# Last stages of three groups moved into the last group's recurrence, with its key-value products on GpSimd

## The reference, cut to what matters

```python
def step(s, rkvw):
    r_t, k_t, v_t, w_t = rkvw
    a = k_t[..., :, None] * v_t[..., None, :]          # product of keys and values
    out = jnp.einsum('bhi,bhij->bhj', r_t, u * a + s)
    s = a + w_t[..., :, None] * s
    return (s, out)
...
x1 = x + og * g @ Wo.T
xc = _ln(x1, ln2_w, ln2_b)
sx2 = jnp.concatenate([state[:, 0:1] - xc[:, :1], xc[:, :-1] - xc[:, 1:]], axis=1)
xk2 = xc + sx2 * ffn_maa_k
xr2 = xc + sx2 * ffn_maa_r
rr = jax.nn.sigmoid(xr2 @ Wfr.T)
kk = jnp.square(jax.nn.relu(xk2 @ Wfk.T))
return x1 + rr * (kk @ Wfv.T)
```

## Time and profile before

| | us |
|---|---|
| median of the runs | 2015.81 |
| the profiled execution, whole | 2021.98 |
| its span, first to last instruction | 2020.2 |
| TensorE (PE) busy | 1784.4 (88%) |
| VectorE (DVE) busy | 1176.1 (58%) |
| ScalarE (ACT) busy | 637.1 (32%) |
| GpSimd (POOL) busy | 223.3 (11%) |
| mean granted TensorE clock | 0.92 |

### The profile page before, as it was taken

The page is one execution under the profiler, slowest core; times in us unless marked ns, Lnnn a source line. Parts: engine busy times, 40 slices in busy tenths (PEclk is TensorE's granted clock), DMA queues, the critical chain, the costliest instruction groups (busy, mean ns, idle before and its releaser), DMA issues.

```text
span 2020.2 us, 18127 instructions
## 1 busy us (share of the span) xinstructions
PE 1784.4 (88%) x6760; PEld 883.8 (44%) x6760; DVE 1176.1 (58%) x1649; ACT 637.1 (32%) x1480; POOL 223.3 (11%) x317
## 2 busy tenths in 40 slices
PE   6999998999999979999999979989779889856447
PEld 3555443445554433455554433445434334422223
DVE  1233002339988853449988654279988633299951
ACT  2566211136652112246641131256621131101011
POOL 1010000122210010122110010221200101100000
PEclk9999998799999989899999988999979987967868
DMA  7000021151102122341102321430012312400011
GB/s 234 26 26 21 22 83 63 62 160 33 40 27 77 63 99 81 96 125 40 53 14 71 105 76 60 128 97 32 14 34 84 103 47 85 146 25 21 7 57 39
DMA packets 73608, 135.15 MB, mean 67 GB/s; under 512 B 16241, under 2 KB 26993, under 8 KB 73521
## 3 DMA queue, kind: packets, MB, share of 16 engines
q1 hardware_dynamic: 59808, 101.05, 15.6%
q0 software_dynamic: 10496, 29.34, 4.7%
q10 hardware_dynamic: 3216, 3.60, 0.6%
HBM read 111.95 MB, written 22.02 MB: 66 GB/s over the span
## 4 chain that ended last, share of the span: by engine, by line
PE 68%; DVE 19%; issue 5%; DMA 3%; ACT 2%; ACTq 1%; POOL 1%; SPq 0%; DVEq 0%; POOLq 0%
PE bank L270 48%; PE bank L433 10%; DVE C L1079 5%; PE bank L497 3%; DVE sm L1020 3%; DVE C L1069 2%; PE bank L312 2%; DMA ring<-in_stream 2%; DVE YB L1091 1%; PE bank L304 1%; DVE C L1083 1%; DMA s<-in_ctx 1%; PE bank L324 1%; ACT XA L809 1%; PE bank L511 1%
## 5 line engine op out<-in xcount | busy, mean ns | idle before, releaser
L270 PE MATMUL bank<-C,ring 128*128 128x448 f32 x640 | 265.2, 577 | 17.9 <-DVE C L1131 17.9
L1079 DVE TENSOR_TENSOR_SCAN C<-XA,C 128x896 f32<-128x896 f32 x112 | 222.6, 2022 | 27.5 <-ACT XA L843 27.5
L433 PE MATMUL bank<-ring,HT 128*112 128x512 f32 x512 | 222.3, 592 | 0.0
L1020 DVE CUSTOM_DVE_ANT_0 sm<-bank,maskb 112x375 f32<-112x375 f32 x256 | 124.0, 541 | 166.5 <-PE bank L304 166.5
L270 PE MATMUL bank<-ctx_t,Wk 128*128 128x375 f32 x512 | 194.3, 504 | 13.4 <-DMA Wk<-in_wk 11.0
L270 PE MATMUL bank<-SX,ring 128*128 128x448 f32 x512 | 196.8, 543 | 7.8 <-ACT SX L809 7.8
L270 PEld LDWEIGHTS bank<-C,ring 128*128 128x128 f32 x640 | 128.5, 203 | 153.5 <-issue 149.6
L270 PE MATMUL bank<-Wv,ctx_t 128*125 128x512 f32 x384 | 182.3, 600 | 0.4 <-ACT C L809 0.4
L270 PE MATMUL bank<-ring,C 128*112 128x512 f32 x256 | 129.5, 662 | 56.1 <-issue 43.6
L312 PEld LDWEIGHTS bank<-ident,sm 112*125 112x125 f32 x768 | 123.5, 192 | 122.5 <-ACT sm L824 59.1
L830 ACT ACTIVATE probT<-bank 125x336 f32<-125x336 f32 x256 | 114.0, 445 | 145.8 <-PE bank L312 143.4
(11 more groups left out here) (132 smaller groups left out, 2056.4 us busy)
## 6 DMA issues: line engine op xcount, KB each, us to landing
ring<-in_stream SPq DMA_DIRECT2D x64, 1024.0 KB, 5.5
ctx_t<-in_ctxT SPq DMA_DIRECT2D x16, 750.0 KB, 5.0
rkw_scratch<-HT POOLq DMA_DIRECT2D x48, 224.0 KB, 2.7
rkw<-rkw_scratch POOLq DMA_DIRECT2D x32, 224.0 KB, 3.1
HT<-in_x SPq DMA_DIRECT2D x16, 224.0 KB, 5.3
X<-in_x SPq DMA_DIRECT2D x16, 224.0 KB, 6.1
v_scratch<-HT POOLq DMA_DIRECT2D x16, 224.0 KB, 2.6
VB<-v_scratch SPq DMA_DIRECT2D x4, 896.0 KB, 7.1
```

The source lines that it names most:

```text
L270: last_ = nc.tensor.matmul(out_ap, pairs[k][0], pairs[k][1], start=(k == 0), stop=(k == len(pairs) - 1))
L433: last_ = nc.tensor.matmul(bank[SC[b]][0:LQ, :], HT[:, c, b * LQ:(b + 1) * LQ], w[:, c, :], start=(m == 0 and c == 0), stop=(m == 3 and c ...
L1020: nc.vector.tensor_tensor_reduce(out=sm[0:LQ, slot, :], in0=tile(name)[0:LQ, 0:LK], in1=maskb[:, n % 2, :], scale=-SCALE, scalar=3.0e38, o ...
L1079: own.step(nc.vector.tensor_tensor_scan(out=part, data0=wrep[:, i % 2, :], data1=part, initial=0.0, op0=ALU.mult, op1=ALU.add))
```

## The change

Four things change.

1. **The last stage leaves the borders.** The borders of groups 1, 2 and 3 keep only WO and the start of `pre`. For groups 0 and 1, x1 is stored to DRAM (`x1_scratch`) in place of the output, and loaded again later; the x1 of group 2 stays in SBUF. The normalised rows of `pre` get four tiles, so that they need not wait for each other, and W1 reads C[1].
2. **The last stages stand elsewhere.** They are done in the order LAST = [2, 0, 1, 3]. Numbers k below count in that order. Layer norm, mixes and FK of k = 0 stand within `pre(3)`; the table AHEAD places the rest of k = 0, and all of k = 1 and 2, between the channels of group 3's recurrence on TensorE (FV of k = 2 behind it); VectorE, ScalarE and GpSimd have their shares at fixed channels. k = 3 follows at the end, with FR ahead of FV rather than in turn with it. These stages use buffers of their own: Wk, Wv, Wq, Wc, qT, V and ctx_t, which are free by then. The normalised rows are made by ScalarE with a third small GpSimd operation (`shift`).
3. **GpSimd makes the products of keys and values in the last recurrence**, up to two channels ahead; VectorE waits for `kv_ready` in place of L1069. The final sum of the last stage is GpSimd's for k < 3.
4. ScalarE's copies of the decays during the MLP are spread in finer portions.

```diff
+LAST = [2, 0, 1, 3]
...
 def pieces_of(g):
+    if g == NG:
+        return [(kind, k) for k in range(NG) for kind in (["wo"] if k == NG - 1 else []) + ["fk", "fr", "fv"]
+                if (kind, k) != ("fk", 0)]
+    return MLP_P + ([("wo", 0)] if g > 0 else []) + PRE_P[0:2] + ([("fk", 0)] if g == NG - 1 else []) + PRE_P[2:4]
...
+AHEAD = {0: [("fr", 0, 0), ("fr", 0, 1), ("fr", 0, 2), ("fr", 0, 3)], 1: [("fv", 0, 0), ("fv", 0, 1)],
+         2: [("fv", 0, 2), ("fv", 0, 3), ("ln", 1)], 4: [("fk", 1, 0), ("fk", 1, 1)], 5: [("fk", 1, 2), ("fk", 1, 3)],
...
+         12: [("fr", 2, 0), ("fr", 2, 1)], 13: [("fr", 2, 2), ("fr", 2, 3)],
+         RS: [("fv", 2, 0), ("fv", 2, 1), ("fv", 2, 2), ("fv", 2, 3)]}
...
+            def border(g):
...
+                w = weights(g, ("wo", 0))
+                pe.wait_ge(og_ready, g)
+                recurrence_out(g, w, 0)
+                recurrence_out(g, w, 1)
+                pre_cols(g, 0)
+                pre_cols(g, 1)
+                recurrence_out(g, w, 2)
+                pre_cols(g, 2)
+                pre_cols(g, 3)
+                recurrence_out(g, w, 3)
...
                     channels_out([("P", g, j, e) for e in range(E)], w, C[j % 2])
+                    if g == NG - 1 and j == 1:
+                        last_cols(0)
+                    elif g == NG - 1 and j == 2:
+                        last_stage(g, [("fk", 0, e) for e in range(E)])
 
             def sum_channels(p):
...
                 for i in range(RS):
+                    last_stage(p + 1, AHEAD.get(i, []))
                     pe.wait_ge(scan_step, p * RS + i + 1)
...
+            def last_product(i):
+                p = NG - 1
+                pool.wait_ge(rkw_in[(i // BLOCK) % 2], 32 * (p * (RS // BLOCK // 2) + i // BLOCK // 2 + 1))
+                if i == 1:
+                    ready(pool, ("P", p, 4, E - 1))
+                elif i >= 4:
+                    pool.wait_ge(summed, i - 3)
+                kk = rkw[:, (i // BLOCK) % 2, i % BLOCK, 1, :]
+                nc.gpsimd.tensor_tensor(S_of[i % 4][:, :, 1:LQ], VB[:, :, 0:LQ - 1],
+                                        kk[:, 0:LQ - 1].unsqueeze(1).to_broadcast([P, RS, LQ - 1]), ALU.mult
+                                        ).then_inc(kv_ready, 1)
...
+                    pool.wait_ge(v_in, 80 * NG)
+                    last_product(0)
+                    last_product(1)
+                    for i in range(RS):
+                        if i in (1, 7):
+                            last_std(1 if i == 1 else 2)
+                        blocks_after(p, i * UNITS, (i + 1) * UNITS)
+                        if i + 2 < RS:
+                            last_product(i + 2)
+                        if i in (2, 9):
+                            last_add(0 if i == 2 else 1)
+                            last_store(0 if i == 2 else 1)
...
             def scan_unit(p, unit):
+                    if last:
+                        dve.wait_ge(kv_ready, i + 1)
+                    else:
+                        own.step(nc.vector.tensor_tensor(S[:, :, 1:LQ], VB[:, :, 0:LQ - 1],
...
+                    for i in range(RS):
+                        if i in (1, 7):
+                            last_stats(1 if i == 1 else 2)
+                        if i in (2, 3):
+                            last_out(0, 2 * (i % 2), 2 * (i % 2) + 2)
+                        elif i in (9, 10):
+                            last_out(1, 2 * ((i + 1) % 2), 2 * ((i + 1) % 2) + 2)
+                        if i in (4, 10):
+                            last_mixes(1 if i == 4 else 2)
+                        units(p, i * UNITS, (i + 1) * UNITS)
```

More of the change, by code:

```diff
@@ L388, in step, with weights, piece_done, channels_out @@
                     denominators(n)
-            def weights(g, k):
-                at = PIECE0[g] + k
+            def weights(g, piece):
+                at = PIECES.index((g, piece))
                 pe.wait_ge(ring_in[at % SLOTS], (at // SLOTS + 1) * 16)
                 return ring[:, at % SLOTS, :, :]
-            def piece_done(g, k):
-                piece_over[PIECE0[g] + k] = (psum_ready, tiles.done)
-            def channels_out(names, w, src, blocks=None):
+            def piece_done(g, piece):
+                piece_over[PIECES.index((g, piece))] = (psum_ready, tiles.done)
+            def channels_out(names, w, src):
                 for e in range(E):
                     k = wide()
[L401 to L406, removed]
+                    closed(product(bank[k][:, 0:T], [(w[:, c, e * P:(e + 1) * P], src[:, c, :]) for c in range(E)]),
+                           names[e], k)
             def mlp(g):
@@ L479, in pre @@
             def pre(g):
-                w0 = 8 if g == 0 else 12
-                if g == 0:
-                    ln_cols("pre", g)
                 k = wide()
@@ L565, in _ @@
                     mlp(g)
+                    border(g)
+                    pre(g)
                 else:
                     sum_channels(g - 1)
-                if g > 0:
-                    post(g)
-                if g < NG:
-                    pre(g)
+                    w = weights(g, ("wo", NG - 1))
+                    pe.wait_ge(og_ready, g)
+                    for b in range(GB):
+                        recurrence_out(g, w, b)
+                    piece_done(g, ("wo", NG - 1))
+                    last_stage(g, [("ln", NG - 1), *((kind, NG - 1, at) for kind in ("fk", "fr", "fv")
+                                                     for at in range(4))])
         @block.sync
@@ new lines, in last_keys @@
+            def last_keys(k, lo=0, hi=E):
+                for e in range(lo, hi):
+                    name = ("FK", k, e)
+                    if k > 0:
+                        ready(act, ("FV", k - 1, GB - 1))
+                    ready(act, name)
+                    nc.scalar.activation(KK[:, e, :], tile(name)[:, 0:T], ACT.Relu).then_inc(freed(name), 1)
+                for e in range(lo, hi):
+                    evacuated(act, ("FK", k, e))
+                    nc.scalar.activation(KK[:, e, :], KK[:, e, :], ACT.Square).then_inc(kk_ready, 1)
@@ new lines, in mlp_add, with pre_apply @@
+            def mlp_add(g, b):
+                name, rows = ("ACC", g, b), rows_of(g, b)
+                ready(dve, name)
+                nc.vector.tensor_tensor(rows, tile(name)[0:LQ, :], rows, ALU.add).then_inc(freed(name), 1)
+                evacuated(dve, name)
+                stats("pre", rows, b)
+            def pre_apply(g, b):
+                dve.wait_ge(rstd_ready["pre"], g * GB + b + 1)
+                nc.vector.tensor_scalar(xn_pre[b], rows_of(g, b), mv["pre"][:, b, 0:1], rstd["pre"][:, b:b + 1],
+                                        ALU.subtract, ALU.mult).then_inc(xn_ready["pre"], 1)
```

472 lines of the change are left out of this document (282 added, 190 removed), and 2 rows, old and new, of the table AHEAD.

## The result

The changed kernel takes 1942.7 us (median of 4 runs, 1927.39 to 1952.98), the kernel before, on the same chip, 2018.86 us (4 runs, 2010.25 to 2030.77): ratio 0.9613, 95% interval 0.9529 to 0.9696. The forecast was 1958 us. The profiled execution is the longest of its four, 1952.98 us with a span of 1951.1 us; the one profiled of before has 2021.98 and 2020.2 us.

A forecast was written before the change was run, and what follows sets the result against it. TensorE was taken to bound the borders, VectorE the last recurrence. From the profiled 2020.2 us: -153 + 26 + 72 - 4 = 1961 us span, 1958 us as median forecast; range 1905 to 2000 (own range 1930 to 1985).

The forecast's parts named there:

- Part 1: Borders of groups 1 to 3: from WO to W1B's end 28.7 us each, in all 153 us less.
- the 2 us for mixes that pace the products: At each border, W1 and W1B paced by mixes take 2 us beyond their 6.29 us, so 8.3 us.
- Part 2: Inside `pre(3)`: P2 starts 13.1 us later and FK of k = 0 adds 13.2 us, 26 us more.
- Part 3: Last recurrence: GpSimd's products count in full on VectorE's path; 208.5 us against 136, 72 us more.
- the 2.3 for the change of hands: Last recurrence: a tenth of a us at each change between VectorE and GpSimd, 2 to 3 us, summed as 2.3.
- counting only half of the statistics and PSUM products: Last recurrence: of 12.4 us on VectorE half counted, 6.2, since a GpSimd product can run beside them; bounds 0 and 12.4.
- the rule for two operands in SBUF: Skill page: a VectorE instruction with two SBUF inputs contends with GpSimd reading SBUF; one with a single input mostly does not.
- Part 4: The end, behind the last recurrence: about 4 us less, bounds -8 and +3.
- A: Rival, last recurrence: VectorE and GpSimd work side by side, about 150 us in place of 208, whole 1900 us; chance 0.08.
- B: Rival, last recurrence: TensorE stays at its lower level, 1.2 GHz; 39 us more than 208, whole 1997 us; chance 0.07.
- C: Rival, last recurrence: GpSimd's product far dearer than its elements, 10.9 us each, 107 us more, whole 2065 us; chance 0.04.
- D: Rival, last recurrence: GpSimd product of 6 to 7.8 us, or waits between small operations and scans; 1987 to 2015 us; chance 0.07.

The follow-up runs named there:

- second profile of the changed kernel: The changed kernel run and profiled once more with no edit, beside three experiments on one chip: 1940.54 us, ratio to the kernel before 0.9594.

## Why the prediction was right

**Part 1, borders: right in kind, 8 us too small.** The forecast was 28.7 us each, measured are 25.7, 25.6 and 27.0: 161 us gone, not 153. Two terms were too large. The first product behind the XA copy was put at 20.3 us from WO's start (18.1 + 2.2) and came at 18.6 us (at 19.9 in group 3). The sum began from group 3's WO of 16.94 us for every border, where group 1's had taken 15.54. And the 2 us for mixes that pace the products were 0.8: W1 and W1B take 7.07 us in place of 6.29. Against these sizes stands that the borders of before aren't fixed to better than 2 us: in the trace of before with GpSimd's products, the same code there, groups 1 and 3 take 81.4 and 79.1 us, not 78.8 and 81.1.

One thing was put at nothing and may not be nothing: WO of group 1 starts at 722.4 and 721.6 us in the two traces with the old code, and between 713.4 and 719.4 in all eight with the new. Which of the edits ahead of it brings these 2 to 9 us, part 4 of the change or another, was not tested.

**Part 2, `pre(3)`: right.** The forecast was 16.3 us between P1 and P2 and 26.3 in all. The trace has 16.7 us (13.6 more than before) and 12.2 of FK, 25.8; the whole stretch from P1's end to the first channel grew by 24.4 us, and another order took 26.1 off. The 8.4 us for normalising and evacuation, 0.5 more than the two terms it was added up from (2.4 and 5.47), were 8.9. The chain named there (evacuation, `last_mixes(0)` on VectorE, LR's bank) is the one in the rows: VectorE's `last_mixes(0)` ran from 1564.81 to 1571.85, its reading of LR's first bank followed, and the wait ahead of P2 is ended by VectorE.

**Part 3, the last recurrence: right, 206.0 against 208.5 us, partly by luck, since two errors cancel.** The first is the size of GpSimd's products. One takes 3.94 to 3.97 us, not 4.2. The Trainium skill, page "GPSIMD Engine Reference", section "3.1 Elementwise — side-by-side cycle accounting", gives 4497 ns for a sum of 2048 elements; by it the prediction had estimated 3.9 us. The measured duration agrees with it better than with the prediction's own 4.2 us from the sum of 512 elements. The experiment with VectorE's own products needs 176.6 us; taking out these 16 products (16 x 1.92 = 30.7) leaves 145.9, so GpSimd's products take 60.1 us of VectorE's path in the changed kernel, 3.8 each, in place of the predicted 67.7 and the 2.3 for the change of hands: 10 us less.

The second is the added work. Of the 176.6 us, 16 x 8.47 = 135.6 are the channels, so it costs 41 us where the prediction put 33.6. VectorE's timeline in that experiment splits them:

| | forecast, us | measured, us |
|---|---|---|
| `last_mixes`, twice | 14.6 | 14.5 |
| statistics and products from PSUM | 6.2 | 11.6 |
| VectorE held by the sums of `last_add` | 9.8 | 8.8 |
| VectorE waiting for FV (1.60 + 2.74 + 1.66) | 0 | 6.0 |
| small GpSimd operations | 3 | about 0 |

So two terms failed: counting only half of the statistics and PSUM products, and putting the hand-over from TensorE at nothing. In this experiment no product of GpSimd stands beside the former; in the changed kernel two of the eight products from PSUM lie beside one, 1.4 us, and no statistics. With GpSimd's products the waits are 2.04, 3.46 and 2.74 us (second profile of the changed kernel). The assumption that a product from PSUM can run beside GpSimd is right all the same: the one at 1771.55 took 0.69 us inside a GpSimd product from 1769.82 to 1773.79. One reading was loose: the 1.26 us in place of 0.17 that the prediction gives beside the rule for two operands in SBUF are a copy's, which has one; the copy of 3.90 us at 1639.62 shows again that copies are held too.

**Part 4, the tail: right within its spread.** 113.3 us before, 109.7 and 107.0 after, forecast 109. The parts were sized wrong in both directions. From WO's start to FK are 28.5 us (26.9 in the second profile) in place of 24.3, where the forecast had 3.5 more and 2 less for a warmer WO (16.98 and 15.35 us for WO, 16.07 before). From FK's start to the end of the last FV are 42.1 (41.3) in place of 49.6: 7.5 less, where the forecast had the wait of 5.28. The experiment gives only 2.4 of it to the order; what shortened the rest of that wait was not tested.

**The sum:** by the stretches measured, 2020.2 - 161 + 24 + 70 - 4 = 1949 us, 2 us under the span of 1951.1; the difference lies in the stretches between them. The forecast of 1961 us for the span was 10 us too long, 8 of them from part 1. In the median it is off by 15 us (1958 against 1942.7): the other 5 come from the profiled execution, which lies 10.3 us above the median of its kernel, where the forecast allowed 5.

**The rivals.** A (side by side) fell in both directions: adding the products alone to the kernel before makes the recurrence 27.8 us longer, removing them from the changed kernel 29.4 us shorter. B (TensorE at its lower level) fell: TensorE is busy for 152.87 of 206 us at a granted clock of 0.86. C and D's dearer product fell by the 3.95 us, D's waits by the 206 us in all.

Why was the change still a gain? It gives 161 us at borders where TensorE was the bound, and takes 70 + 24 back. Of these 94 us, 29 are the products on GpSimd, 24 the place of k = 0 in `pre(3)`, and only the rest, 41, is the price of the moved stages in a window where VectorE is the bound.

## What to carry to other kernels

Before moving work from VectorE to GpSimd, find one place in the trace where a GpSimd operation on SBUF overlaps a VectorE operation with two SBUF operands. If the durations that both have by themselves add up to the time from first start to last end, the move is worth VectorE's duration minus GpSimd's, here 1.92 - 3.95, a loss, even though GpSimd ran up to two channels ahead (measured: 29.4 us for 16 products, 1.8 each). Work moved out of a stage bounded by one engine into one bounded by another is priced there by the second engine's time, plus its waits where the first engine hands results over, here 6.0 of 41 us. The place of the moved work in the stage where it starts needs its own look: 24 us here hung on where the transposes and the 16 products of one moved stage stood. Where executions differ by more than the part in question, measure from a fixed event in the trace to the next.

## What the runs showed of the hardware that was not expected

A VectorE instruction that is held may stay held through several GpSimd instructions, and even a short one may be held long. Timelines of VectorE and GpSimd in the changed kernel:

```profile
1666.51 9.70 DVE L1227 SCALAR_TENSOR_TENSOR bon<-rkw,ucol 128x112 f32<-128x112 f32 x1
...
1665.74 3.97 POOL L794 TENSOR_TENSOR HT<-VB,rkw 128x1776 f32<-128x1776 f32 x1
1669.66 3.96 POOL L794 TENSOR_TENSOR C<-VB,rkw 128x1776 f32<-128x1776 f32 x1
1673.57 2.49 POOL L777 TENSOR_TENSOR X<-X,ctx_t 112x512 f32<-112x512 f32 x2
```

VectorE's product of 112 elements, 0.33 us by itself, ends with the last of four GpSimd instructions, at 1676.2. In the pair shown first the engines took turns instead: scan, GpSimd's product, scan, GpSimd's product, VectorE's product. What decides between the two was not found. At the start of the recurrence the copy of 16 elements per partition, 0.17 us by itself, took 3.90 us and the sum behind it 3.95, one GpSimd product each, behind 3.85 us of waiting for the first product, so VectorE's first scan starts 12.0 us after the channel's first instruction. The Trainium skill, page "SBUF — State Buffer", section "Who interferes with whom", says that whoever issues first gets the shared ports for the whole instruction; the turns agree with that, the 9.70 us need more, and the page says nothing of what follows a wait.

The holding goes both ways. A small operation of GpSimd on one element, 0.57 us by itself, took 2.13 us beside a scan. Timeline of GpSimd in the changed kernel, the same line twice:

```profile
1737.12 0.57 POOL L764 TENSOR_TENSOR rstd_post<-vare_post,half 112x1 f32<-112x1 f32 x1
...
1738.58 2.13 POOL L764 TENSOR_TENSOR rstd_post<-vare_post,half 112x1 f32<-112x1 f32 x1
```

And executions of the same code differ ahead of the places that were edited. Of the eight products ahead of P1 and P1 itself, the changed kernel's profile has 6.34 and 13.86 us, that of `pre(3)` in another order 3.27 and 12.29, in the timelines of PE above. The granted clock over the eight products, from 1535.8 to 1542.1 and from 1525.8 to 1529.0, is 0.50 in the one and 1.00 in the other, the two levels of TensorE's clock (1.2 and 2.4 GHz). This one place accounts for 4.6 us of the 14.6 us between them at the end of P1.
